# Where a hidden sort runs: its last 61 pieces moved into the second attention, and the closing norm spread over three engines

## The reference, cut to what matters

```python
# layer 1, attention: 8 heads of 8, each token sees 31 neighbours of its own parity
attn = softmax(einsum(q, k_neighbours) * scale);  h = h + (attn @ v) @ w_proj + b_proj
# layer 1, experts: one pair of experts per sequence, from the mean of its tokens
x = layernorm(h)
out = w1 * expert_1(x) + w2 * expert_2(x)
h = h + (layernorm(out + x) * gamma + beta)
# layer 2, experts: a graph layer over 262144 edges, which needs the edges sorted by target
```

## Time and profile before

| | us |
|---|---|
| median of 3 runs | 5984.23 |
| the runs | 5978.08 to 5991.55 |
| the profiled execution, its own time | 5975.13 |
| its span, first to last instruction | 5973.4 |
| mean granted TensorE clock | 0.906 of full |

### The profile page before, as it was taken

The page is one execution under the profiler, slowest core; times in us unless marked ns, Lnnn a source line. Parts: engine busy times, 40 slices in busy tenths (PEclk is TensorE's granted clock), DMA queues, the critical chain, the costliest instruction groups (busy, mean ns, idle before and its releaser), DMA issues. The chain is left out here.

```text
span 5973.4 us, 109087 instructions
## 1 busy us (share of the span) xinstructions
PE 4928.8 (83%) x39929; PEld 3337.0 (56%) x39929; DVE 4706.3 (79%) x8677; ACT 2491.8 (42%) x4448; POOL 2671.6 (45%) x3019
## 2 busy tenths in 40 slices
PE   5477978987546999999699999999994579958998
PEld 3463225655424666666577777777773127842452
DVE  6896998888686888888578888888886677767667
ACT  4353443333325666666333333333332452222332
POOL 0000001000324676787567777777775701015557
PEclk9787998999667999999799999999997789968999
DMA  0300000011322111000112222222221000030252
GB/s 18 85 1 6 8 23 21 29 36 45 85 65 45 19 25 24 3 2 2 28 35 44 43 44 45 46 44 44 44 43 29 10 1 3 3 75 20 71 132 44
DMA packets 269134, 208.07 MB, mean 35 GB/s; under 512 B 139498, under 2 KB 242835, under 8 KB 267571
## 3 DMA queue, kind: packets, MB, share of 16 engines
q1 hardware_dynamic: 195806, 145.14, 8.7%
q0 software_dynamic: 72912, 57.02, 6.4%
q10 hardware_dynamic: 12, 0.39, 0.0%
HBM read 113.55 MB, written 69.40 MB: 31 GB/s over the span
## 5 line engine op out<-in xcount | busy, mean ns | idle before, releaser
L3514 PE MATMUL edges_bank<-part_room,hot_room 128*128 128x512 f32 x6656 | 1526.4, 391 | 76.0 <-ACT XT L3537 56.4
L3514 PEld LDWEIGHTS edges_bank<-part_room,hot_room 128*128 128x128 f32 x6656 | 1248.4, 188 | 354.1 <-ACT XT L3537 68.6
L3493 POOL DMA_INDIRECT XT<-gat_node_table,edges_idx x1216 | 1202.3, 989 | 392.5 <-issue 308.7
L3537 ACT COPY XT<-edges_bank 128x512 f32<-128x512 f32 x832 | 474.7, 597 | 656.3 <-PE edges_bank L3514 560.8
L3632 DVE COPY_PREDICATED XT<-edges_tabs_p,XT 128x1024 f32<-128x1024 int32 (+7 forms) x768 | 576.2, 750 | 38.3 <-DVE edges_acc_s L3681 7.1
L3613 DVE TENSOR_SCALAR hot_room<-edges_lanes,edges_nodes 128x512 fp32r<-128x512 f16 (+1 forms) x768 | 350.6, 517 | 169.3 <-PE edges_bank L3514 85.0
L505 POOL TENSOR_TENSOR X<-H,ln_f_mean 128x1024 f32<-128x1024 f32 x5 | 11.4, 2279 | 910.1 <-DVE ln_f_shift L542 910.1
L1837 ACT ACTIVATE GT<-attc_sc,attc_nm 128x256 f32<-128x256 f32 x1024 | 399.5, 480 | 31.0 <-DVE attc_nm L1915 31.0
L1915 DVE TENSOR_REDUCE attc_nm<-attc_sc 128x4 f32<-128x1024 f32 x256 | 313.0, 1223 | 108.9 <-PE attc_sc L1756 108.9
L1851 ACT ACTIVATE GT<-attc_sct 128x1024 f32<-128x1024 f32 x256 | 262.0, 1024 | 303.7 <-PE attc_sct L1767 303.6
L1756 PE MATMUL attc_sc<-XT,attc_tT 64*128 64x256 f32 x2048 | 295.2, 407 | 44.6 <-ACT GT L1837 44.6
(11 more groups left out here) (858 smaller groups left out, 10165.1 us busy)
## 6 DMA issues: line engine op xcount, KB each, us to landing
gat_states<-GT SPq DMA_DIRECT2D x32, 768.0 KB, 3.4
XT<-gat_node_table,edges_idx POOLq DMA_INDIRECT x1216
edges_lanes<-gat_places SPq DMA_DIRECT2D x128, 128.0 KB, 3.1
expert_pairs<-in_L_ffn_W_dram SPq DMA_DIRECT2D x48, 256.0 KB
edges_lanes<-gat_places SPq DMA_DIRECT2D x64, 160.0 KB, 3.2
XT<-XT SPq DMA_DIRECT2D x32, 256.0 KB
XT<-XT SPq DMA_DIRECT2D x64, 128.0 KB
XT<-XT SPq DMA_DIRECT2D x128, 64.0 KB
```

The lines of the kernel that those rows point to most:

```text
L3493: nc.gpsimd.indirect_dma_start(out=rows[:, k, c, :], out_offset=None, in_=q.t_table, in_offset=bass.IndirectOffsetOnAxis(ap=idx[:, k, c:c ...
L3514: m = nc.tensor.matmul(banks[t][:], hot[:, (k * GROUPS + j) % 2, b, t, :], parts[:, p, b].rearrange("p u c -> p (u c)"), start=b == 0 and ...
L3537: nc.scalar.copy(fetched[:, (k * GROUPS + j) % 2, t].rearrange("p u c -> p (u c)"), banks[t][:]).then_inc(fetched_in, 1)
```

## The change

Attention 1 takes 189 pieces (three in each of its first 63 sequences), the experts of layer 1 none. Exchanges between rows 4, 8 and 16 apart are made on DVE by `stream_shuffle` inside the merge piece, and their transfers are gone. In attention 1 the reciprocal becomes Ln and Exp on ACT, the product is made an iteration later, after the maxima, one of the three pieces runs ahead of the maxima and two behind, and DVE takes the statistics of each finished sequence. `ln_f1` takes the form `known=True`. In the expert stage DVE takes the statistics of `X`, and POOL adds beta into `H`, one 128x128 addition a sequence. The new `closing_norm` splits the eight groups over DVE, ACT and POOL.

```diff
@@ a new function @@
+def closing_norm(nc, g, name, x, gamma, stored):
+
+    HT, N2 = 16, D // 2
+    BY_DVE, BY_ACT, BY_POOL = (0, 3, 7), (1, 4, 6), (2, 5)
...
+                sp.dma_start(gam[:], gamma.partition_broadcast(P)).then_inc(params, 16)
+                sp.wait_ge(stored, 48)
...
+                def norm(n):
+                    s = group(n)
+                    link(vec.tensor_tensor(x[:, s, :], x[:, s, :], bc(mean[:, s], 2, D), ALU.subtract))
+                    link(vec.tensor_tensor(x[:, s, :], x[:, s, :], bc(rstd[:, s], 2, D), ALU.mult))
+                def close(n):
+                    s = group(n)
+                    link(vec.tensor_tensor(x[:, s, :], x[:, s, :], bc(gam[:], 1, HT), ALU.mult))
+                    vec.tensor_tensor(g.H[:, s, :], x[:, s, :], g.H[:, s, :], ALU.add).then_inc(closed, 1)
+                even, odd = g.stats[:, :, 1], g.stats[:, :, 4]
...
+                link(vec.reciprocal(rstd[:], std[:]))
+                vec.scalar_tensor_tensor(shift[:], mean[:], -1.0, rstd[:], ALU.mult, ALU.mult).then_inc(scaled, 1)
+                v.wait_ge(params, 16)
+                for k, n in enumerate(BY_DVE):
+                    norm(n)
+                    close(n)
+                    v.wait_ge(normed_a, k + 1)
+                    close(BY_ACT[k])
+                v.wait_ge(closed, len(BY_DVE) + len(BY_ACT))
+            @block.scalar
+            def _(act):
+                act.wait_ge(var_ready, 1)
+                nc.scalar.activation(std[:], var[:], ACT.Sqrt, bias=g.eps[:], scale=1.0 / D).then_inc(std_ready, 1)
+                act.wait_ge(scaled, 1)
+                for n in BY_ACT:
+                    for t in range(n * HT, (n + 1) * HT):
+                        m = nc.scalar.activation(x[:, t, :], x[:, t, :], ACT.Identity, bias=shift[:, t:t + 1], scale=rstd[:, t:t + 1])
+                    m.then_inc(normed_a, 1)
+            @block.gpsimd
+            def _(pool):
+                gp, done = nc.gpsimd, 0
+                pool.wait_ge(params, 16)
+                pool.wait_ge(scaled, 1)
+                for n in BY_POOL:
+                    s = group(n)
+                    for other, op in ((bc(mean[:, s], 2, D), ALU.subtract), (bc(rstd[:, s], 2, D), ALU.mult), (bc(gam[:], 1, HT), ALU.mult)):
+                        gp.tensor_tensor(x[:, s, :], x[:, s, :], other, op).then_inc(pool_own, 1)
+                        done += 1
+                        pool.wait_ge(pool_own, done)
+                    gp.tensor_tensor(g.H[:, s, :], x[:, s, :], g.H[:, s, :], ALU.add).then_inc(closed_p, 1)
+                pool.wait_ge(closed_p, len(BY_POOL))
@@ -2004,6 +2082,7 @@
     HEADS, DH, NEIGHBOURS = 8, 8, 31
+    SORT_ROUNDS = HIDDEN["attb"] // SORT_A_ROUND
     SETS, GROUPS, ROWS = 2, 4, 32
@@ -2056,7 +2135,7 @@
                 for b in range(B):
-                    for _ in range(HIDDEN["attb"] // B):
+                    for _ in range(SORT_A_ROUND if b < SORT_ROUNDS else 0):
                         g.order.sync(sp)
@@ -2203,9 +2282,19 @@
-                for i in range(-AHEAD - 1, B):
+                nc.scalar.preload_act_table_set("natural_log_exp_and_others")
+                def invert(b):
+                    act.wait_ge(spread, b + 1)
+                    nc.scalar.activation(total[:], total[:], ACT.Ln).then_inc(logged, 1)
+                    act.wait_ge(logged, b + 1)
+                    nc.scalar.activation(total[:], total[:], ACT.Exp, scale=-1.0).then_inc(inverted, 1)
+                for i in range(-AHEAD - 1, B + 1):
                     if 0 <= i < B:
                         exps(i)
+                    if 0 <= i - 1:
+                        invert(i - 1)
                     if i + AHEAD + 1 < B:
@@ -2233,15 +2322,21 @@
-                def normalize(b):
+                def spread_sums(b):
                     v.wait_ge(o_moved, b + 1)
                     vec.stream_shuffle(total[:], o[:, b % 2], [ONES + n % ONES for n in range(ROWS)]).then_inc(spread, 1)
-                    v.wait_ge(spread, b + 1)
-                    vec.reciprocal(total[:], total[:]).then_inc(inverted, 1)
+                def normalize(b):
                     v.wait_ge(inverted, b + 1)
...
                     vec.tensor_tensor(oT[:, b % 2].rearrange("p (j u) -> p u j", u=2), o[:, b % 2], total[:], ALU.mult).then_inc(normed, 1)
+                def measure(b):
+                    v.wait_ge(misc_read, b + AHEAD + 3)
+                    for t in range(b * TPB, (b + 1) * TPB):
+                        m = vec.bn_stats(g.stats[:, t, :], g.H[:, t, :])
+                    return m
@@ -2259,10 +2354,15 @@
                 for i in range(-AHEAD - 1, B + 1):
+                    hidden = SORT_A_ROUND if 0 <= i + AHEAD < SORT_ROUNDS else 0
+                    for _ in range(hidden // 2):
+                        g.order.vector(v)
                     if 0 <= i + AHEAD < B:
                         maxima(i + AHEAD)
-                        for _ in range(HIDDEN["attb"] // B):
-                            g.order.vector(v)
+                    if 0 <= i - 1:
+                        normalize(i - 1)
+                    for _ in range(hidden - hidden // 2):
+                        g.order.vector(v)
                     v.wait_ge(misc_full, i + AHEAD + 2)
@@ -2273,8 +2373,10 @@
                     if 0 <= i < B:
-                        normalize(i)
-                v.wait_ge(misc_read, B + AHEAD + 1)
+                        spread_sums(i)
+                    if 0 <= i - 2:
+                        measure(i - 2)
+                link(measure(B - 1))
@@ -2556,7 +2658,7 @@
-def sequence_experts(nc, g, name, pairs, Wr, br, b1, b2, target, hide):
+def sequence_experts(nc, g, name, pairs, Wr, br, b1, b2, target, hide, beta):
@@ -2567,6 +2669,8 @@
         rev = st.sb("rev", [B, E])
+        bet = st.sb("beta", [P, D])
+        shifted_h = st.sem("shifted_h")
         mean = st.sb("mean", [P, B])
@@ -2606,6 +2711,7 @@
                                allow_small_or_imprecise_dtypes=True).then_inc(made, 1)
+                pool.wait_ge(loaded, 112)
                 pool.wait_ge(pairs.built, 16 * pairs.BUILDS)
@@ -2614,10 +2720,12 @@
                         in_offset=bass.IndirectOffsetOnAxis(ap=idx[:, b:b + 1], axis=0)).then_inc(gathered[b % NB], 16)
+                    h = g.H[:, TPB * b:TPB * b + TPB, :]
+                    nc.gpsimd.tensor_tensor(h, h, bc(bet[:], 1, TPB), ALU.add).then_inc(shifted_h, 1)
...
             def _(pe):
-                pe.wait_ge(loaded, 96)
+                pe.wait_ge(loaded, 112)
                 pe.wait_ge(mean_ready, 1)
@@ -2712,7 +2820,7 @@
                 vec.tensor_scalar(mean[:], mean[:], 1.0 / S, None, ALU.mult).then_inc(mean_ready, 1)
-                v.wait_ge(loaded, 96)
+                v.wait_ge(loaded, 112)
                 v.wait_ge(product, 1)
@@ -2760,6 +2868,12 @@
+                def measure(b):
+                    v.wait_ge(y_added, b + 1)
+                    for t in range(TPB * b, TPB * b + TPB):
+                        m = vec.bn_stats(g.stats[:, t, :], target[:, t, :])
+                    return m
                 done = 0
@@ -2769,15 +2883,18 @@
                         add(i - 3)
-                v.wait_ge(y_added, B)
+                    if 0 <= i - 4:
+                        measure(i - 4)
+                link(measure(B - 1))
+                v.wait_ge(shifted_h, B)
...
-    turned_norm(nc, g, "ln_f1", g.H, keep=g.X)
-    sequence_experts(nc, g, "expb", pairs, I["L1_ffn_Wr"], I["L1_ffn_br"], I["L1_ffn_b1"], I["L1_ffn_b2"], g.X, HIDDEN["expb"])
+    turned_norm(nc, g, "ln_f1", g.H, keep=g.X, known=True)
+    sequence_experts(nc, g, "expb", pairs, I["L1_ffn_Wr"], I["L1_ffn_br"], I["L1_ffn_b1"], I["L1_ffn_b2"], g.X, HIDDEN["expb"], I["L1_ffn_beta"])
     lane_of_nodes(nc, g, q, g.order)
-    layernorm(nc, g, "ln_out1", g.X, I["L1_ffn_gamma"], I["L1_ffn_beta"], add=g.H, drained=(g.order.stored, 48))
+    closing_norm(nc, g, "ln_out1", g.X, I["L1_ffn_gamma"], g.order.stored)
@@ -2786,7 +2903,9 @@
 SAMPLES = 32
-HIDDEN = {'atta': 64, 'expa': 128, 'attb': 128, 'expb': 61}
+SHUFFLED, LANES = (2, 3, 4), 32
+HIDDEN = {'atta': 64, 'expa': 128, 'attb': 189, 'expb': 0}
+SORT_A_ROUND = 3
@@ -2804,13 +2923,15 @@
         self.stored, self.lanes_ready, self.searched = st.sem("stored"), st.sem("lanes_ready"), st.sem("searched")
+        self.shuffled, self.shuffles = st.sem("shuffled"), 0
         row_bits, levels = ROW.bit_length() - 1, EDGES.bit_length() - 1
...
         def exchange(h, b):
-            swaps[h] += 16 * len(self.partners(b))
+            if b not in SHUFFLED:
+                swaps[h] += 16 * len(self.partners(b))
             return swaps[h]
@@ -2903,7 +3024,12 @@
             else:
-                v.wait_ge(self.swapped[part], swaps[0])
+                if b in SHUFFLED:
+                    self.shuffles += 1
```

(42 more changed lines are left out.)

## The result

The changed kernel takes 5882.93 us (median of 4 runs, 5872.68 to 5890.25), the kernel before 5985.04 beside it (5978.08 to 5991.55): a ratio of 0.9834 with an interval of 0.982 to 0.9848, or 102 us less. Predicted were 5904 with a range of 5880 to 5940. The profiled execution of the changed kernel took 5872.68 us, its span is 5871.0, against 5973.4 before.

The account below looks back on a forecast made before the run. Stages run one after another behind barriers, so kernel time is their sum. Closing norm -29.2, `ln_f1` -9.7, experts' loop -22 and attention 1 -19 make -80: median 5984.2 becomes 5904 us, range 5880 to 5940.

Parts of the forecast that it names:

- the likeliest case: Whole kernel: comes out as forecast, 5904 us, within its own range of 5890 to 5918; chance 0.57.
- The experts' loop: Second expert stage: without sort pieces POOL sets the pace at 1.85 us a sequence, 128.2 against 150.3, -22 us.
- The clock rival: Experts' loop: PE stays at 1.2 GHz for half of it, 24 us longer, kernel 5928 us; chance 0.17.
- Attention 1: Second attention: plain rounds 509, shuffles 27 and leftover transfers 4 make 540 against 559.2 us, -19 us.
- The plain round: Attention 1, a round without exchanges: 8.08 us, set by the way through both engines, not DVE's own 7.66.
- The 4 us left for transfers: Attention 1: stalls kept for exchanges 1, 2, 32 and 64 apart, which stay on transfers; 4 us.
- The shuffles: Attention 1: 24 shuffles of 128x1024 at 1.22, 1.29 with semaphore, add 27 us to the rounds; bounds 9 and 36.
- The closing norm: Closing norm split over DVE, ACT and POOL, each POOL pass costing DVE 1.66: 39.0 against 68.2 us, -29.2.
- that rival falls: Closing norm: DVE and POOL take no turns, DVE's passes stay at 1.2, 13 us less, 5891; chance 0.05.
- `ln_f1`: This norm takes the form of `ln_f3`: 28.3 against 38.0 us, -9.7 us.
- Table loads: Attention 1: Ln and Exp make ACT reload its tables, +60 us, 5964, still faster than before; chance 0.03.
- the slower case: Attention 1: PE's clock falls in rounds with shuffles and stays low, +120 us, 6024, slower than before; chance 0.03.

Follow-up runs that it names:

- Experiment 6: The changed kernel without the addition of beta in the second expert stage (output lacks beta): 5875.8 us in one run.
- Experiment 9: The changed kernel with the move undone, two sort pieces a sequence in attention 1 and 61 in the experts' loop, shuffles kept: 5878.03 us, ratio 0.9831.
- experiment 4: The changed kernel with the closing norm on DVE and ACT only, four groups each, no POOL: 5872.18 us, ratio 0.9813.
- experiment 8: The changed kernel with two sort pieces ahead of attention 1's maxima, one behind, and the closing norm without POOL: 5861.05 us, ratio 0.9808.
- experiment 1: The changed kernel with two sort pieces ahead of the maxima and one behind in attention 1, in place of one and two: 5864.46 us, ratio 0.9801.
- Experiment 5: The changed kernel with the first exchange of attention 1's pieces (4 apart) back on SP's transfers: 5872.53 us in one run.
- experiment 2: The changed kernel with attention 1's reciprocal back on DVE, no Ln and Exp on ACT: 5955.81 us in one run.
- experiment 7: The changed kernel with 24 sequences' beta added by POOL ahead of the gathers, as three 128x1024 additions: 5881.32 us in one run.
- experiment 3: The changed kernel with the exchanges 4, 8 and 16 rows apart back on transfers, no shuffles: 5941.33 us in one run.

## Why the prediction was nearly right

The sum was -80 and the kernel gained 102 (in the median as in the profiled execution). Sign and stages were right, and 5882.9 lies in the range; it lies 7 us under the likeliest case's own range of 5890 to 5918, and 3 us above the lower end of the whole range. The 22 us come from one term above all.

- **The experts' loop, the step that was mis-sized: -36.4 where I had -22.** The cause is right as far as it goes: no merge holds DVE, PE does not stand still and its clock stays up for longer. Experiment 6 also measures PE's pace at full clock, 1.49 for the 1.5 estimated. Experiment 9 shows a part that the prediction did not have: beside pieces POOL's own work takes 2.11 a sequence. The pace was wrong: 1.61 a sequence for 1.85, worth 15 us. I had added 0.6 for the addition to the whole of 0.95 and 0.30. But the 0.30 is a gap behind a gather, 0.30 in experiment 6, of which only 0.17 is left with an addition in it. Gather and addition are 0.97 + 0.47 + 0.17 = 1.61, so the addition costs 0.36. The 4.6 for six sequences at the lower clock did not come: the clock was at half until 1523.0, but POOL had six buffers to fill and kept its pace (the first periods behind the first are 1.61 to 1.63). Four later ones cost 4 together. The end of the pipeline is 9.4 instead of 7. And the 150.3 began at the second gather, 1.5 us into the loop. Together 15.1 + 4.6 - 4 - 2.4 + 1.5 = 14.8 of the 14.4 missing.
- **The clock rival (0.17) did not come in its size.** Behind the loop's start half clock held for 10.2 us and 4 gathers in the changed kernel, for 20.5 us and 8 in experiment 4, for 3.4 us and one in experiment 8, and not at all in experiments 1 and 5. It costs 0 to 8 us, not 24.
- **The end of experts A was missed: -3.7.** I looked for SP's transfers only where DVE and PE wait for them. SP also issued 16 ahead of the barrier for the next stage's first exchange. Experiment 5 puts these transfers back and the 3.9 us with them.
- **Attention 1, -21 where I had -19.** The plain round is 8.08, as worked out, and experiment 1 shows that it goes through the addition. The 15 rounds with exchanges lie 27.7 us above it, for 27 predicted in 14. This is in part luck: two rounds of both merges behind the maxima take 11.57 and 12.23 for the 10.66 worked out, with PE at half clock in them, and most others are 0.1 to 0.2 shorter than worked out. The 4 us left for transfers are not there: no wait for XT<-XT or for the row copies is left in the stage. Outside of the row copies the stage is 3.5 longer (47.2 against 43.7). The table load is not what explains it: with the same load the first row copy of experiment 9 comes 28.3 us into the stage, as before the change (28.4), and here 29.7. My figure for DVE's own round, 7.66, was wrong (7.40, experiment 2) without effect on the plain rounds, which DVE's own work does not set.
- **The shuffles: 1.30 each for 1.22 to 1.29 taken.**
- **The closing norm, -27.2 where I had -29.2.** The turns are there, so that rival falls. POOL's passes with gamma and with `H` are 3.20 long, where I had taken all as those of `ln_f3`, 2.76, and a turn costs DVE by so much more: (1676.9 - 1640.25 - 18 x 1.19) / 8 = 1.9 instead of 1.66. In `ln_f3` four DVE passes stood beside POOL's, not five as the rival's sentence has it, which changes nothing. Experiment 4 measures what the turns cost: without POOL 6.7 us less. In experiment 7 an operation of 0.20 takes 2.18 beside POOL's. The Trainium skill, page "SBUF — State Buffer", section "SBUF: two separate sides", says that whichever of the two engines starts first keeps the shared ports for its whole instruction. Experiments 4 and 7 agree with a turn of that length; that these ports are the cause is the page's word, no run separates it.
- **`ln_f1`, -11.2 where I had -9.7.** Its length is 26.9 here and 28 in half of the other kernels.
- **Table loads and the slower case**: one load in the stage (L2285), so that rival is out. The slower case is out in its size only: PE's clock did fall in two rounds with shuffles and just behind them, for 3.4 us each, but it came back each time, and the stage's mean is 0.96.

What the prediction did not see is how the parts share the gain. The move that the change is named after costs 36.4 us in attention 1 and gives back 33.3 in the expert stage (experiment 9). These are single profiles, but both ratios agree: 0.9834 and 0.9831. The whole gain is there without the move: 57.4 in attention 1, 27.2 in the closing norm, 10.0 in `ln_f1`, 3.7 at the end of experts A and 3.1 in the expert stage. In attention 1 it is above all the stalls that the shuffles remove (64 us in experiment 3).

The 74 us of experiment 2 must be read with care. They are what the reciprocal on DVE costs with three pieces a sequence, where DVE has 0.55 idle in a round. With two pieces the kernel before had it on DVE and a plain round of 7.92, and experiment 9 has it on ACT and one of 7.82. So without the move the swap is worth about 0.1 a round or some 6 us, by my estimate from these two rounds; no run has two pieces, the shuffles and the reciprocal on DVE. It makes room for the third piece, and the third piece pays nothing.

Still open: why PE's clock falls in some runs of the loop and not in others with the same pace.

## What to carry to other kernels

In a pipeline over two engines write down every ring, not only each engine's own work: here 7.40 (DVE), 7.82 (maxima and scores) and 8.08 (through the addition), and only the longest pays when it is cut, down to the next. Test each part of a change on its own, and with and without the others: this one's name-giving part was neutral, and the 74 us of another hold only beside it. A share given to POOL beside a busy DVE was paid for by DVE here, and beside POOL's large additions even tiny operations of DVE were.

## What the runs showed of the hardware that was not expected

- A gather issued by POOL takes 0.95 to 0.97 us beside an idle or lightly used DVE and 1.24 beside sort pieces (1.29 before the change, where that set its 1.60). The Trainium skill, page "DMA: Bandwidth & Descriptors", section "SWDGE vs HWDGE vs iDMA", says that POOL writes the descriptors into SBUF, where DVE locks it out during its two-port modes. That the gathers are longer beside DVE's pieces fits this; no run shows which lock it is, or that the pieces run in such a mode.
- Of the 0.30 us between two gathers about half vanishes when another POOL instruction stands there: addition and gaps together are then 0.47 + 0.17.
- PE's clock fell to half in the middle of the experts' loop in some executions (10.2 us in the changed kernel, 20.5 in experiment 4) and in others of the same pace not at all (experiments 1 and 5).
- POOL's addition of 128x1024 with beta spread over 16 tiles took 2.31 (6.93 for three) beside small DVE work; in the closing norm, in turn with DVE, 2.74 to 3.20.
